# Two dense row tiles between the steps of each group of a graph layer's scattered sums

## The reference

```python
xn = layernorm(x)
agg = segment_sum(edge_weight * xn[dst], src)            # 53125 edges into 3125 rows
gnn = agg @ W.T + b
q, k, v = xn @ Wq, xn @ Wk, xn @ Wv                      # 8 heads of 32
Q, K, v = elu(q) + 1, elu(k) + 1, v / L
KV = einsum('nshd,nshv->nhdv', K, v)
Z = 1 / (einsum('nlhd,nhd->nlh', Q, K.sum(1)) + 1e-6)
msg = einsum('nlhd,nhdv,nlh->nlhv', Q, KV, Z) * L
msg = layernorm(msg @ Wm, g1, b1)
h = relu(concat([xn, msg]) @ W1) @ W2                    # 512 -> 512 -> 256
mix = xn + layernorm(h, g2, b2)
x = x + gnn + mix
n3 = layernorm(x); logits = n3 @ gate_w + gate_b         # 16 experts, top 2
x = x + sum over 2 chosen experts of gate * (silu(n3 @ w1) * (n3 @ w2)) @ w3
```

## Time and profile before

| what | us |
|---|---|
| three timed runs | 1555.85, 1557.48, 1558.01 (median 1557.48) |
| profiled execution, its own time | 1554.42 |
| span of its trace | 1552.6 |
| groups 1 to 10, 240.5 to 789.07 | 548.6 |
| groups 11 and 12, 789.07 to 862.36 | 73.3 |
| dense layers up to the logits, 862.36 to 1103.15 | 240.8 |

### The profile page before, as it was taken

One profiled execution on the slowest core, in us unless ns is written; L12 is line 12 of the kernel. 1 busy time (PEld: TensorE's weight loads), 2 busy tenths in 40 slices (PEclk: granted clock), 3 DMA queues, 4 the chain that ended last, 5 costly groups with the idle time before them and its releaser, 6 DMA issues.

```text
span 1552.6 us, 24067 instructions
## 1 busy us (share of the span) xinstructions
PE 1207.1 (78%) x7172; PEld 1010.1 (65%) x7172; DVE 960.4 (62%) x2681; ACT 357.6 (23%) x881; POOL 574.9 (37%) x587
## 2 busy tenths in 40 slices
PE   0589776776677677677789999999239999999990
PEld 0466455654565465455544888998229999999990
DVE  2962388888888888888989565544752222222225
ACT  0455231132033113203300343334111111111110
POOL 1420477657447545644752000000033333333320
PEclk9889987998999899899899999999559999999995
DMA  3211233323223222322321000000058999999967
GB/s 118 67 35 34 71 104 104 94 79 92 66 68 101 68 69 82 89 65 69 104 69 43 1 1 17 17 17 17 15 180 292 332 334 331 336 331 332 335 219 254
DMA packets 118265, 196.07 MB, mean 126 GB/s; under 512 B 13421, under 2 KB 67499, under 8 KB 118187
## 3 DMA queue, kind: packets, MB, share of 16 engines
q1 hardware_dynamic: 92074, 123.82, 24.0%
q0 software_dynamic: 26112, 71.34, 14.8%
HBM read 177.12 MB, written 17.99 MB: 126 GB/s over the span
## 4 chain that ended last, share of the span: by engine, by line
PE 58%; DVE 22%; issue 6%; DVEq 6%; DMA 3%; POOL 2%; SPq 2%; ACT 1%; ACTq 0%; POOLq 0%
PE psum L891 15%; PE psum L733 8%; PE psum L901 7%; PE psum L748 6%; PE psum L799 6%; PE psum L658 5%; DVE agg L1076 4%; PE psum L807 3%; DVE agg L1082 2%; DVE record L988 2%; PE psum L679 2%; POOL arena L582 2%; DVE in_tile L982 2%; DVE hot L1064 2%; DVEq L1091 1%
## 5 line engine op out<-in xcount | busy, mean ns | idle before, releaser
L582 POOL DMA_INDIRECT arena<-y_rows,gather_i x416 | 403.0, 969 | 334.3 <-DVEq L1011 131.5
L733 PE MATMUL psum<-arena,hot 128*128 128x256 f32 x832 | 265.8, 461 | 142.1 <-DVE hot L1064 83.2
L733 PEld LDWEIGHTS psum<-arena,hot 128*128 128x128 f32 x832 | 169.1, 224 | 228.5 <-DVE hot L1064 126.3
L392 ACT ACTIVATE in_slot<-iota,place_f 128x128 f32<-128x128 f32 x416 | 126.9, 387 | 450.8 <-DVE place_f L977 398.9
L748 PE MATMUL psum<-arena,hot 128*128 x624 | 161.8, 395 | 38.5 <-DVE hot L1069 35.1
L1076 DVE TENSOR_TENSOR agg<-psum,agg 128x256 f32 x416 | 175.9, 423 | 18.2 <-PE psum L733 17.2
L891 PEld LDWEIGHTS psum<-arena 128*128 128x128 f32 x1536 | 181.1, 194 | 4.9 <-issue 2.5
L891 PE MATMUL psum<-arena 128*128 128x128 f32 x1536 | 181.6, 277 | 1.9 <-DVE arena L1373 1.9
L1380 DVE TENSOR_TENSOR arena<-psum,arena 128x512 f32<-128x512 f32 x64 | 44.3, 692 | 202.8 <-PE psum L891 202.8
L748 PEld LDWEIGHTS psum<-arena,hot 128*128 128x128 f32 x624 | 109.0, 190 | 80.7 <-issue 70.9
L1064 DVE TENSOR_SCALAR hot<-iota,node_in_bin,weight 128x128 f32<-128x128 f32 x416 | 145.1, 354 | 24.3 <-issue 24.2
(11 more groups left out here) (199 smaller groups left out, 1608.3 us busy)
## 6 DMA issues: line engine op xcount, KB each, us to landing
arena<-in_L_ffn_w_dram SPq DMA_DIRECT2D x144, 512.0 KB, 5.7
xnT<-in_L_ffn_w_dram SPq DMA_DIRECT2D x48, 512.0 KB
arena<-y_rows,gather_i POOLq DMA_INDIRECT x416, 2.8
arena<-chosen_rows SPq DMA_DIRECT2D x8, 640.0 KB, 9.1
agg<-in_x_dram SPq DMA_DIRECT2D x4, 640.0 KB, 11.1
y_rows<-arena SPq DMA_DIRECT2D x4, 640.0 KB, 3.4
n_rows<-arena SPq DMA_DIRECT2D x4, 640.0 KB
out_dram<-agg SPq DMA_DIRECT2D x4, 640.0 KB
```

Of the source, the lines that this page charges most:

```text
L392: act.activation(in_slot[k % 2][:, c, :], iota[:, :], ACT.Abs, bias=place_f[:, k * CH + c:k * CH + c + 1])
L582: pool.indirect_dma_start(rows[h][:, t, :], None, y_rows, bass.IndirectOffsetOnAxis(ap=gather_i[h][:, t:t + 1], axis=0)).then_inc(gathered ...
L733: pe.matmul(bank_of(g, t // 2)[:, (t % 2) * C:(t % 2 + 1) * C], hot[:, n % HOTS, :], rows[h][:, t, :], start=True, stop=True).then_inc(met, 1)
```

## The change

The dense work is laid into the groups. Group g carries the tiles 2g and 2g + 1 (group 12 one tile) through query to residual; `beside(g, step)` on TensorE and on VectorE says at which of the 56 steps each part stands, the sorting of group g + 2 among them. The pair's tiles are computed together in banks 4, 5 and 6. Query and ELU of pair g + 1 stand in group g, so that ScalarE's table changes to Exp and back once per group, near its end. The stages of the third norm and the gate become a pass over all 25 tiles after the last group.

Further: LEAD is 6 instead of 4. The columns of the cross one-hots are no longer read through registers: TensorE transposes the list (`turn_list`), multiplies it with a matrix that marks each bin's tile (`pick_list`), and VectorE copies the result (`keep_picked`). All 32 bin registers of a group are loaded at the end of the group before (`bins_named`), and list_ready is given only after them. TensorE reads its row registers at the group's start. The records are made at steps 23, 28, 36 and 43, and the reorders stand at 31, 37, 44 and 51.

The lead, and the order on TensorE; further down in the same function stand hidden(g, 0) to hidden(g, 3) at steps 27, 29, 33 and 35, query(g + 1) at 39 and down at 42 and 46:

```diff
-    LEAD = 4
-    MLOAD = 16
+    LEAD = 6
...
+            def beside(g, step):
+                sorts, more = g + 2 < NG, g + 1 < NG
+                if step == 4:
+                    attend(g)
+                if step == 5 and more:
+                    turn_list(g + 1)
+                if step == 8 and more:
+                    pick_list(g + 1)
+                if step == 11:
+                    turn_tok(g, d_msg, d_msgT)
+                if step == 13 and sorts:
+                    prefix(g + 2)
+                if step == 15:
+                    merge(g)
+                if step == 24:
+                    turn_tok(g, d_n1, d_n1T)
...
+            def hidden(i, m):
+                w = len(pair_of(i)) * P
+                if m == 0:
+                    pe.wait_ge(d_n1T_kept, i + 1)
+                for k in range(2 * KC):
+                    operand = xnT[:, k, 2 * i * P:2 * i * P + w] if k < KC else feat[:, k - KC, 0:w]
+                    last = pe.matmul(bank[5 + m // 2][:, m % 2 * w:(m % 2 + 1) * w], w1[:, k, m * P:(m + 1) * P], operand,
+                                     start=(k == 0), stop=(k == 2 * KC - 1))
```

VectorE, whose own `beside` has message at step 6, keep_picked at 10, pair_stats at 18, first_norm at 21, query_elu(g + 1) at 47, pair_stats at 49 and residual at 53; the group's end; and the pass after the groups:

```diff
+            def pair_stats(n, i, produced, b):
+                dve.wait_ge(produced, i + 1)
+                for j in range(len(pair_of(i))):
+                    dve.bn_stats(stat[:, n, j, 0:6], bank[b][:, j * C:(j + 1) * C])
+                dve.drain()
...
                 if g + 2 < NG:
                     make_list(g + 2)
+                if g + 1 < NG:
+                    its_bin = bins_named(g + 1)
+                if g + 2 < NG:
+                    dve.sem_inc(list_ready, 1)
...
+            for i in range(TURNS + 1):
+                if i < TURNS:
+                    x_stats(TURNS + i)
+                if i >= 1:
+                    x_root_of(TURNS + i - 1)
+                    for t in range((i - 1) * U, i * U):
+                        dve.tensor_scalar(n3[:, t, :], agg[:, t, :], x_stat[:, t, 6:7], x_root[:, 1, t:t + 1],
+                                          ALU.subtract, ALU.mult).then_inc(n3_ready, 1)
```

More of the change, by code:

```diff
@@ new lines, in attend @@
+            def attend(i):
+                w = len(pair_of(i)) * P
+                pe.wait_ge(d_elu, i + 1)
+                if i == 0:
+                    pe.wait_ge(kvd_ready, 1)
+                for j in range(len(pair_of(i))):
+                    for m in range(KC):
+                        last = pe.matmul(bank[5 + j][:, m * (P + HPC):(m + 1) * (P + HPC)], q_elu[:, m * w + j * P:m * w + (j + 1) * P],
+                                         KVd[:, m, :], start=True, stop=True)
+                last.then_inc(d_att, 1)
@@ new lines, in down @@
+            def down(i, j):
+                if j == 0:
+                    pe.wait_ge(d_relu, 2 * i + 2)
+                for k in range(HC):
+                    last = pe.matmul(bank[4][:, j * C:(j + 1) * C], relu_h[:, k, j * P:(j + 1) * P], w2[:, k, :],
+                                     start=(k == 0), stop=(k == HC - 1))
+                if j == len(pair_of(i)) - 1:
+                    last.then_inc(d_down, 1)
+            def beside(g, step):
[14 more added lines that the diff above has]
+                    turn_tok(g, d_n1, d_n1T)
+                if step == 27:
+                    hidden(g, 0)
+                if step == 29:
+                    hidden(g, 1)
+                if step == 31 and sorts:
+                    reorder(g + 2, 0)
+                if step == 33:
+                    hidden(g, 2)
+                if step == 35:
+                    hidden(g, 3)
+                if step == 37 and sorts:
+                    reorder(g + 2, 1)
+                if step == 39 and more:
+                    query(g + 1)
+                if step == 42:
+                    down(g, 0)
+                if step == 44 and sorts:
+                    reorder(g + 2, 2)
+                if step == 46 and len(pair_of(g)) == 2:
+                    down(g, 1)
+                if step == 51 and sorts:
+                    reorder(g + 2, 3)
@@ L725, in add_up @@
                 pe.wait_ge(list_ready, g + 1)
+                _, row_of = nc.values_load_multi_w_load_instructions(
+                    cross_row[h][0:1, :], engines=PE, min_val=0, max_val=GT - 1,
+                    skip_runtime_bounds_check_because="tiles are clipped when the list is made")
                 for t in range(GT):
@@ L734, in add_up @@
                               start=True, stop=True).then_inc(met, 1)
-                    if g + 2 < NG and t == 12:
-                        prefix(g + 2)
-                    if g + 2 < NG and t == 28:
-                        reorder(g + 2, 0)
-                _, row_of = nc.values_load_multi_w_load_instructions(
-                    cross_row[h][0:1, :], engines=PE, min_val=0, max_val=GT - 1,
-                    skip_runtime_bounds_check_because="tiles are clipped when the list is made")
+                    beside(g, t)
                 for b in range(CROSS):
@@ L1059, in _ @@
             make_list(1)
+            first_bins = bins_named(0)
+            dve.sem_inc(list_ready, 1)
             def hot_row(g, t):
@@ L1089, in add_up @@
                 for t in range(GT):
-                    if t % MLOAD == 0:
-                        _, its_bin = nc.values_load_multi_w_load_instructions(
-                            bin_of[h][0:1, t:t + MLOAD], engines=DVE, min_val=0, max_val=BINS - 1,
-                            skip_runtime_bounds_check_because="a tile's first edge lies in a bin")
-                    if t == GT - LEAD:
-                        _, col_of = nc.values_load_multi_w_load_instructions(
-                            cross_col[h][0:1, :], engines=DVE, min_val=0, max_val=GT,
-                            skip_runtime_bounds_check_because="tiles are clipped when the list is made")
                     if t + LEAD < GT:
```

649 lines of the change are left out of this document (303 added, 346 removed).

## The result

The changed kernel takes 1545.6 us (median of 5 runs, 1538.4 to 1548.3) against 1557.5 before (5 runs, 1554.8 to 1558.0): ratio 0.992, 95% interval 0.990 to 0.994, 11.8 us faster. The forecast was 1504, 53 us faster: the direction is right, four fifths of the gain are missing.

The account below looks back on a forecast made before the run. VectorE was taken to bound the groups and TensorE the dense layers; -216.3 + 135.5 + 6 + 20 + 1.5 = -53.3 us takes the profiled 1554.4 to 1501, median 1504 us; eight in ten: 1435 to 1560.

Parts of the forecast that it names:

- dense stage out, pass in: The 240.8 us dense stage leaves; a 24.5 us pass over 25 tiles replaces it: -216.3 us.
- The period: List to list in groups 1 to 10: 68.4 us against 54.86, VectorE waiting for TensorE in steps 24 to 47.
- TensorE's 15 us for the same steps fit beside it: Steps 0 to 21 of a group: VectorE's 25.0 us set the pace and TensorE's work hides beside them.
- The new pass: Third norm and gate after the last group: VectorE at 0.85 us a tile sets the pace, 24.5 us in all.
- The upper bound of 36: Third-norm pass: 36 us if TensorE at half clock sets the pace.
- The last two groups: Groups 11 and 12, which sort nothing ahead: 93.5 us instead of 73.3, +20 us.
- Group 0 and the prologue: Group 0 +6 us, its gathers hiding half the added work; prologue +1.5, TensorE waiting for the turned list on ScalarE.
- Rival A: Groups: the queues even out, VectorE is the only bound; period 60.5 us, median 1413 us; chance 0.21.
- B: Groups: ScalarE's slot one-hots hold up TensorE; period 79 us, 1610 us; chance 0.11 together with D.
- C: Groups: TensorE stays at 1.2 GHz through steps 24 to 47; +26.6 us per group, about 1770 us; chance 0.02.
- D: Groups: no overlap, the dense work merely moves; 78 us per group, 1600 us; chance 0.11 together with B.
- Gathers. No cost.: 32 gathers per group, 40 us of 68, issued one group ahead; list_ready 2.5 us later costs nothing.

Follow-up runs that it names:

- e1: Changed kernel with 8 of the 16 hidden-layer matmuls per pair left out (output wrong): 1859.5 us, 0.993 of the kernel before.
- e2: Changed kernel with both down projections moved behind the group's last cross, their statistics and residual into the next group: 1864.2 us, 0.996 of the kernel before.
- f3: The kernel of e2 once more, beside the control f1: 1865.6 us, 0.991 of the kernel before.
- f2: Changed kernel's same instructions reordered, TensorE's work spread over the whole group: 1794.0 us, 0.953 of the kernel before.
- g3: The spread order of f2 again, unaltered, where the kernel before takes 1555 to 1558 us: 1434.2 us, ratio 0.9225.
- h3: Changed kernel with one of each gate's two products left out in the third-norm pass (logits wrong): 1894.9 us, 1.012 of the kernel before.
- h4: Changed kernel with nine filler matmuls before the third-norm pass and a 256-column filler before each tile's turn: 1897.2 us, 1.015 of the kernel before.
- i2: Spread order of f2 with gathers four at a time and 128-column fillers in the third-norm pass: 1507.8 us, 0.8014 of the kernel before.
- e4: Changed kernel with TensorE's prologue reordered: prefix and list turn before the next x tiles, picks after: ratio 1.018 to the kernel before.
- f4: Changed kernel with LEAD 4 instead of 6: 1921.8 us, 1.021 of the kernel before.
- h1: Changed kernel with GpSimd's gathers issued four at a time, on the second kind of chip: 1598.1 us, 0.854 of the kernel before.
- f1: The changed kernel unaltered, as control on the second kind of chip: 1919.2 us, 1.020 of the kernel before.
- before_paced: The kernel before with its gathers issued four at a time, on the first kind of chip: 0.9998 of the kernel before.
- e3: Changed kernel with nine filler matmuls before the third-norm pass and a 64-column filler before each tile's turn: 1915.2 us, 1.021 of the kernel before.

## Why the prediction was right or wrong

The direction was right, the size was not. In microseconds of the profiled execution:

| term | forecast | came |
|---|---|---|
| dense stage out, pass in | -216.3 | -205.6 |
| groups 1 to 10 | +135.5 | +164.0 |
| groups 11 and 12 | +20 | +18.4 |
| prologue and group 0 | +7.5 | +17.5 |
| sum | -53.3 | -5.7 (span: -6.0) |

The forecast misses by 47.6 us: 28.5 in the ten groups, 10.0 in the prologue and group 0, 10.7 in the new pass, less 1.6 in the last two groups.

- **The period, the term that failed most: right in kind, mis-sized.** "Period: 25.0 + 28.3 + 1.7 + 13.4 = 68.4 us" measured 71.3, and the term +135.5 came as +164.0. In the group read (70.7 us) steps 0 to 21 with the registers took 28.8 against 27.5, the stretch 30.9 (570.95 to the last addition at 601.85) against 28.3 + 1.7, the tail 11.0 against 10.9 (13.4 without the registers). In steps 0 to 21 VectorE waits 1.5 us for TensorE, whose queue stands first for VectorE's message (1.76) and the picks (1.18) and works at the low clock; I had let "TensorE's 15 us for the same steps fit beside it", and that is the step of the walk that was wrong. The walk's VectorE work in the stretch adds up to 18.5 us, not to 17 to 18; that leaves 9.8 of waiting, and the waits read there were 9.2. An error of 4% in the period is over half of the forecast gain, because the gain is a difference of two terms, 216 and 136. e1, e2, f3, f2 and g3 show the mechanism itself.
- **The new pass: a step that failed.** The prediction put it as "so it keeps up even at half clock, roughly". By its own 0.7 us a tile, doubled, TensorE would have needed 1.4 against VectorE's 0.85. It measured 1.17 against 0.78. The upper bound of 36 named this case, and the value was taken from the wrong end. h3 shows that TensorE was the pace, h4 and i2 that the clock was the reason. 10.7 us.
- **The last two groups** came out right in sum (91.7 against 93.5), in part by luck: from the list's end the first took 51.5 (to the next group's first one-hot) against 54, the last 40.2 against 39.5.
- **Group 0 and the prologue.** Of the 17.5 us, 5.8 are in the prologue. TensorE does wait for the turned list, as predicted, but e4 shows that this decides nothing, and up to 4 us are scatter. The other 11.7 are in group 0 (+6 forecast); its spread version takes 68.5 us against 78.1, so its late steps pay for the clump too. No run took the gathers out of group 0, so the split isn't settled.
- **Rival A** (period 60.5) is not this kernel, but g3 reaches 61.2 with the same work. **B**: the copies and ReLUs on ScalarE never held TensorE in the group read, and the exponential was done 5.7 us before VectorE wanted it. **C**: the clock rises some 5 us into the stretch (two hidden products take 1.03 us from 575.90 on, two took 1.65 before). **D** would have been 78.
- **LEAD** was named as part of the reason ("at most LEAD (now 6) steps between them"). f4 shows that within the stretch 4 or 6 makes no measurable difference (42.0 against 42.1 us); for the steps before it the lead was tested only where the extra wait lies over them.
- **"Gathers. No cost."** holds on the first kind of chip only. On the second the changed kernel is 2% slower than the kernel before. The prediction had no view that could show it, since the traces before came from the first kind.

## What to carry to other kernels

Averages per engine say what a rearrangement can reach, not what it does: walk both in-order queues step by step, and where one is full and the other waits, move work until the waits thin out before judging the idea (here 12 us became 123). Price a phase of small matmuls at the low clock too, and take that bound unless a trace of such a phase shows the clock held; here it fell in one of them although the pause in front was filled. And when another engine has long waits without a releaser on its core, look at whether they end with GpSimd's gathers; gaps between the gathers took 26 us a group off under one condition and cost nothing under the other.

## What was not expected of the hardware

- In four sets (1869 to 1882 us for the kernel before) the changed kernel's period was 98.4 against 71.3 us: VectorE stood some 27 us a group until the queued gathers were through, and with the gathers four at a time the period was 72.5 (h1). The Trainium skill ("Runtime: NRT & Kernel Launch", Instruction fetch mechanics) has it that the sequencer streams its code by itself and that crossing a block is "mostly hidden". No run here shows otherwise: no instruction packet ends these waits in f1. What does, why the sets differ, and whether the same stall slows the kernel before (before_paced ran on the first kind alone) stay open.
- TensorE's granted clock fell from 1.00 to 0.50 at 1433 us in e3, in turns, gates and fillers of 64 columns, 0.8 us after a wait of 0.49 us, and stayed there for 30 us of a full busy row; with fillers of 128 (i2) or 256 columns (h4) in the same place it stayed at 1.00. The Trainium skill ("TensorE: Matmul & The Clock Gate", Part 1: The HAM clock gate) says that activity releases the throttle. The busy row alone doesn't tell that activity: full for 30 us, it released nothing here.
- 32 registers loaded in one go stop VectorE for 2.25 us, within the bounds of 1.3 to 3.8.
